# Five engines' tile loops written out, or run as hardware loops: a graph attention kernel

## The reference

```python
def transformer_conv(x, src, dst, Wq, bq, Wk, bk, Wv, bv, Ws, bs, H, C, concat):
    q, k, v = (x @ W + b).reshape(n, H, C) for each of (Wq, bq), (Wk, bk), (Wv, bv)
    alpha = einsum('ehc,ehc->eh', q[dst], k[src]) / sqrt(C)
    p = exp(alpha - segment_max(alpha, dst)[dst])
    out = segment_sum(p[:, :, None] * v[src], dst) / (segment_sum(p, dst) + 1e-16)[:, :, None]
    out = out.reshape(n, H * C) if concat else out.mean(axis=1)
    return out + x @ Ws + bs

h = relu(transformer_conv(x, ..., H=4, C=128, concat=True))      # layer 1
y = transformer_conv(h, ..., H=2, C=128, concat=False)           # layer 2
return layernorm(x + y)
```

## Time and profile before

| | |
|---|---|
| median of 3 runs | 2353.86 us |
| the profiled execution: its own time | 2353.86 us |
| its span, first to last instruction | 2352.0 us |
| instructions in the trace | 55216 |
| TensorE products busy | 2138.1 us (91%) |
| VectorE / ScalarE / GpSimd busy | 1650.4 / 1591.5 / 1097.3 us |
| mean granted TensorE clock | 0.972 of full |

### The profile page before, as it was taken

The page is one execution under the profiler, slowest core; times in us unless marked ns, Lnnn a source line. Parts: engine busy times, 40 slices in busy tenths (PEclk is TensorE's granted clock), DMA queues, the critical chain, the costliest instruction groups (busy, mean ns, idle before and its releaser), DMA issues. The chain is left out here.

```text
span 2352.0 us, 55216 instructions
## 1 busy us (share of the span) xinstructions
PE 2138.1 (91%) x16157; PEld 1722.1 (73%) x16158; DVE 1650.4 (70%) x5577; ACT 1591.5 (68%) x3083; POOL 1097.3 (47%) x1476
## 2 busy tenths in 40 slices
PE   2788888888799999999999999997797999999995
PEld 1356666666588888888888888886466888888884
DVE  5689999999567666666666666675236666666664
ACT  1589999999576767767677767775114666666663
POOL 4410000000366666666666666665015666666663
PEclk8889999999899999999999999999798999999998
DMA  2012222222578778878777787775507888889983
GB/s 77 1 43 90 88 89 85 85 85 89 127 152 149 149 149 150 151 149 148 151 149 150 151 149 149 149 143 99 174 1 150 169 174 171 173 168 173 169 168 82
DMA packets 708209, 300.98 MB, mean 128 GB/s; under 512 B 657322, under 2 KB 669254, under 8 KB 707747
## 3 DMA queue, kind: packets, MB, share of 16 engines
q1 hardware_dynamic: 704731, 295.98, 61.0%
q10 hardware_dynamic: 3266, 2.36, 0.4%
HBM read 92.94 MB, written 48.00 MB: 60 GB/s over the span
## 5 line engine op out<-in xcount | busy, mean ns | idle before, releaser
L1227 DVE CUSTOM_DVE_ANT_0 prob_l<-score_l,mask_l 125x512 f32<-125x512 f32 (+2 forms) x1050 | 646.9, 617 | 395.1 <-PE score_l L1333 387.2
L1333 PE MATMUL score_l<-KT,QT_l 128*125 128x512 f16 (+2 forms) x3150 | 772.6, 355 | 4.8 <-DVE piece_max_l L1227 4.6
L1094 POOL TENSOR_TENSOR prob_parts_l<-prob_l,prob_parts_l 125x512 f16<-125x512 f32 x600 | 676.7, 1160 | 16.2 <-ACT prob_parts_l L1167 16.2
L1158 ACT ACTIVATE prob_l<-prob_l,neg_max_l 125x1024 f32<-125x1024 f32 (+1 forms) x450 | 524.3, 1165 | 98.3 <-DVE neg_max_l L1235 98.3
L1173 ACT CAST probT_l<-transposed_l 128x375 f16<-128x375 f32 x450 | 209.9, 466 | 388.9 <-PE transposed_l L1358 388.9
L1365 PE MATMUL output_l<-V,prob_flipped_l 128*125 128x256 f16 x2400 | 471.4, 277 | 0.8 <-DMA prob_flipped_l<-prob_parts_l 0.7
L1082 POOL CAST QT_l<-q_now_l 128x125 f16<-128x125 f32 x150 | 43.4, 290 | 883.6 <-ACT q_now_l L1145 883.6
L751 PE MATMUL mask_banks<-hot,work 125*125 125x313 bf16 x2432 | 387.9, 307 | 61.9 <-DVE hot L658 61.8
L1367 PE MATMUL output_l<-V,prob_flipped_l 128*125 128x128 f16 x2400 | 431.8, 219 | 0.0
L1333 PEld LDWEIGHTS score_l<-KT,QT_l 128*125 128x125 f16 x3150 | 370.2, 138 | 81.4 <-issue 12.1
L751 PEld LDWEIGHTS mask_banks<-hot,work 125*125 125x125 bf16 x2432 | 278.4, 136 | 153.9 <-DVE hot L658 62.7
(11 more groups left out here) (185 smaller groups left out, 2460.9 us busy)
## 6 DMA issues: line engine op xcount, KB each, us to landing
mask_scratch<-work SPq DMA_DIRECT2D x128, 273.4 KB
mask_l<-mask_scratch SPq DMA_DIRECT2D x72, 341.7 KB
mask_l<-mask_scratch SPq DMA_DIRECT2D x24, 683.8 KB
mask_l<-mask_scratch SPq DMA_DIRECT2D x24, 683.4 KB
prob_flipped_l<-prob_parts_l SPq DMA_TRANSPOSE x600, 3.2
mask_l<-mask_scratch SPq DMA_DIRECT2D x24, 342.1 KB
hT_scratch<-rowsT_l SPq DMA_DIRECT2D x25, 250.0 KB, 4.4
hT<-hT_scratch SPq DMA_DIRECT2D x6, 1024.0 KB, 14.5
```

What stands on the lines that cost most here:

```text
L1094: pool.tensor_tensor(parts[0:TP, 1, a:b], prob[:, h % 2, a:b], parts[0:TP, 0, a:b], ALU.subtract).then_inc(s_flo, 1)
L1158: act.activation(e, e, ACT.Exp, bias=neg_max[:, h % 2:h % 2 + 1], accum_out=total[:, h % 2, c:c + 1]).then_inc(s_exp, 1)
L1227: dve.tensor_tensor_reduce(out=prob[:, h % 2, a:b], in0=score_bank(h, p)[0:TP, 0:b - a], in1=mask[:, parity, a:b], scale=1.0, scalar=-3.0e ...
L1333: last = pe.matmul(score_bank(h, p)[0:TP, 0:b - a], QT[:, h % 2, i, :], KT[:, h, j, a:b], start=n == 0, stop=n == len(products) - 1)
```

## The change

In both attentions, every engine's `over_tiles` is given its engine and no longer writes out all tiles. Tile 0 is written out, tiles 1 to 22 run as a hardware loop of 11 passes of two tiles each, with the tile number in a register, and tiles 23 and 24 are written out. The order of the instructions on data, the semaphores, the DMAs and the buffers are the same.

```diff
--- before.py
+++ after.py
@@ -985,10 +985,14 @@
-        def over_tiles(body):
+        def over_tiles(eng, body):
 
-            for t in range(NT):
-                body(t, t // 2, t % 2)
+            body(0, 0, 0)
+            with eng.Fori(0, (NT - 3) // 2) as i:
+                body(2 * i + 1, i, 1)
+                body(2 * i + 2, i + 1, 0)
+            body(NT - 2, (NT - 2) // 2, 1)
+            body(NT - 1, (NT - 1) // 2, 0)
@@ -1069,7 +1073,7 @@
-                over_tiles(tile)
+                over_tiles(sp, tile)
@@ -1135,7 +1139,7 @@
-                over_tiles(tile)
+                over_tiles(pool, tile)
@@ -1201,7 +1205,7 @@
-                over_tiles(tile)
+                over_tiles(act, tile)
@@ -1304,7 +1308,7 @@
-                over_tiles(tile)
+                over_tiles(dve, tile)
@@ -1415,7 +1419,7 @@
-                over_tiles(tile)
+                over_tiles(pe, tile)
```

## The result

The kernel after takes 2394.29 us (median of 4 runs, 2392.74 to 2398.27); the kernel before took 2353.91 us beside it (4 runs, 2352.99 to 2353.97). The ratio is 1.0175, with a 95% interval of 1.0157 to 1.0193: slower by 40.4 us. The profiled execution has a time of 2396.13 us and a span of 2394.3 us, so it lies 42.3 us above the profiled execution of before. Lines of `attention` stand 4 further down than before: L1122 is L1126, L1227 is L1231, L1333 is L1337.

The account below looks back on a forecast made before the run. TensorE was taken to bound both attentions, with no slack in the chain through the maximum. 2353.86 + 7 (registers) + 23 (layer 1 fetches) = 2384 us, branch and table taken as nothing; 8-in-10 range 2356 to 2450.

Parts of the forecast that it names:

- The forecast case: Fetch stalls at the jumps of layer 1 alone, registers small; chance 0.35, own range 2365 to 2400 us.
- (1) Registers: Computing tile-dependent wait values in 132 looped attention steps costs 0.05 us per step, 7 us; bounds nothing to 119 us.
- (2) The branch: Ten taken branches per layer and engine cost 1 us at most on VectorE; TensorE's taken as nothing.
- (3) The fetch: VectorE's layer 1 pass is not kept; each of ten jumps waits 2.3 us for instructions, 23 us; bounds nothing to 53.
- The 1.16 us taken off as covered: After its jump VectorE would wait for the next piece anyway, so 1.16 us of each 3.5 us fetch is hidden.
- The count of 500: VectorE's layer 1 pass was estimated at about 500 instructions, 32 KB or 4 packets; layer 2's at half.
- (4) The table: ScalarE's exponential function table needs no reload in the attention loops, so no cost was taken.
- Fetches at every jump of both layers: Rival: all 20 jumps stall TensorE and VectorE, 4 us each, 80 + 7, giving 2441 us; chance 0.2.
- A table load in every pass: Rival: ScalarE reloads its function table in each of 22 passes, 28 us, giving 2389 or 2412 us; chance 0.2.
- Registers alone: Rival: all passes are kept and only register operations cost, 2354 to 2361 us; chance 0.2.
- Faster, by less fetching: Rival: less instruction fetching returns at most TensorE's 5.9 us of idle time in layer 1, 2348 us; chance 0.05.
- TensorE's queue cannot stay ahead: Sign of predicting too low: with 16% more to read, every attention step is longer, up to 0.9 us.

Follow-up runs that it names:

- e3: Kernel after, with VectorE's queue told at the top of each pass where its closing branch will go; 2359.72 us, ratio 1.0031.
- e1: Kernel after with only VectorE's tile loop kept as a hardware loop, the other four engines written out; 2393.41 us, ratio 1.0178.
- e2: Kernel after with VectorE's tiles all written out, the other four engines looping; 2353.34 us, ratio 1.0005.
- e7: Kernel after with 12 extra products of 384 columns on TensorE at each layer 1 jump, ahead of the awaited scores; 2387.16 us, ratio 1.0147.
- e4: Kernel after with VectorE's layer 1 loop starting on the first instruction of a block of 128; 2393.86 us, ratio 1.0176.
- e8: Kernel after with layer 1 written out and four satisfied waits ahead of each VectorE piece in layer 2's loop, pass of 337 instructions; 2369.12 us, ratio 1.0073.
- e9: Kernel after with layer 1 written out and six satisfied waits ahead of each VectorE piece in layer 2's loop, pass of 393 instructions; 2434.06 us, ratio 1.0347.

## Why the prediction was right, and where its sizes were off

2384 us with a range of 2356 to 2450 stood against 2394.29. The forecast case is what happened: stalls at the ten jumps of layer 1, none in layer 2, registers small. The forecast is 10 us low, in the main by a registers term 3 us too large and a fetch term 14 us too small.

*(1) Registers, 7 us.* In layer 1 the 0.05 us per step are right: 88 steps, 4.4 us (e3's layer 1), half from VectorE and half from the others (e1, e2). In layer 2 it is nothing, 519.9 us against 519.8. The term is about 4 us. Why it is nothing there no run shows. A step of layer 2 is 0.6 us longer; that the queues have more slack there is a guess.

*(2) The branch, nothing.* The branches take 59 ns on VectorE and 208 on TensorE, as in the earlier trace rows, and e2 with four engines' branches costs nothing that the times show.

*(3) The fetch, 10 × 2.3 = 23 us: the term that was mis-sized.* It measured 37.2 us. The mechanism and the place are right: between 916.02 and 919.76 VectorE has nothing to do because of the fetch, and e3 takes it away by the hint alone. Two things in the size were wrong. First, the fetch was priced at 3.5 us, by the landing of transposes. From the start of the piece behind which VectorE jumps (915.54) to the start of the next (919.76) it is 4.22 us. The 1.16 us taken off as covered are right, and 3.06 are left where 2.3 were taken. They reached TensorE nearly whole, as forecast: a jump tile at full clock is 2.8 us longer. The wait in TensorE's list is 2.17 of them; where the other 0.6 lie I haven't traced. Second, TensorE's clock was put at nothing, without a word on it: the same 2.2 us of idling put it at 1.2 GHz for 3.4 us behind eight of ten jumps, 1.1 us each, 9 us, and e7 shows that without the idling they are gone. 10 × 2.8 + 8 × 1.1 = 36.8.

The choice of engine hung on a guess, that a pass of four blocks is too long and one of two is not. It held, but for a reason that I had not given, and so far it was luck. The count of 500 was 431. The packets show that VectorE's queue can hold the whole pass (e3: none fetched), and that without the hint five blocks are fetched where four are touched, the last of them past the loop's end (e4). What fits all eight runs is that this block takes the place of the loop's first one; three blocks and the next one have room together (e8), four and the next one have not (e4, e9). With the hint the block past the end isn't brought, and VectorE stands for it on its way out (e3). That the queue reads on is shown by the times of the packets; that it drops the first block for it is argued, since no row shows what is dropped. Whether the number of instructions decides, or how many blocks they touch, no run tells apart: none has 337 instructions over four blocks. Nor is any other engine's limit measured. TensorE kept about 1500 instructions, ScalarE 200, GpSimd 146 and SyncE 157.

The Trainium skill (Runtime: NRT & Kernel Launch, Instruction fetch mechanics) gives 512 instructions for most engines and 2048 for TensorE, with purely sequential prefetch, and says that a taken branch out of a window of two pages waits for a DMA. By the size alone a pass of 431 would fit, and so would the 500 that the prediction put over the edge by it; the trace says no. With the block behind it, 431 + 128 is above 512, and 337 + 128 is below it. So the runs agree with its size and with its sequential prefetch taken together. Its window of two pages does not agree with TensorE, which jumped back over about 1500 instructions, nearly six of its packets of 16.4 KB, and fetched none.

*(4) The table, nothing.* Two loads, both ahead of the loops.

*The rivals.* Fetches at every jump of both layers: refuted by the empty queues of layer 2. TensorE's pass, the longest, was the one that never had to be fetched. A table load in every pass: refuted by the count. Registers alone: that is what e3 makes of the kernel, 2359.72 us, inside its 2354 to 2361. Faster, by less fetching: e3 fetches nothing over 740 us, and its tiles are 40.79 us against 40.59; the registers take 0.2 us there, and nothing is seen to come back. *TensorE's queue cannot stay ahead*, the way to be wrong low: it did stay ahead, since the waits in TensorE's list are those at the ten jumps and one of 0.4 us.

No run was faster than the kernel before. The version with loops whose time can't be told from before is e2, with VectorE's tiles written out.

## What to carry to other kernels

Before putting a long body into a hardware loop, count each engine's compiled instructions in one pass, register operations included, and not only those of the engine that bounds. A pass of VectorE of 337 jumped back free and one of 393 cost about 4 us a jump on a path with no slack, both with their first instruction at the start of a block; how a pass of 337 does elsewhere in a block no run shows. If the count is above, write that engine's loop out, shorten its pass, or give the hint of the jump back: here the hint took 34.6 of 40.4 us away. A wait of 2.2 us on a saturated TensorE cost 2.8 us here, and 3.9 where the clock fell behind it; take the price of a stall from the tile that contains it, not from the wait.

## What the runs showed of the hardware that I had not expected

- The clock fell after 2.2 us of idling, and not every time: in eight of ten equal jumps, at 0.50 for 3.4 us. With 12 products in the gap it never fell at a jump.
- Five packets a pass are fetched for four blocks, the fifth for instructions that don't run. The hint of the jump removes not only the wait but all of the packets.
- The hint has a price behind the loop: a wait of 3.78 us on VectorE in layer 1, and in layer 2 one of 2.6 us on TensorE.
- Satisfied waits on an engine that idles a third of its time are not free: 28 more a step on VectorE cost 0.31 us a step, 42 more cost 0.82.
